# Overlapping a layer norm and its keys with the first steps of a scan, in a one-core Macaron block

## The chip, the cores and the metric

The kernel runs on one core of a Trainium2 chip. The metric is the device time of one execution, in microseconds (us), as the median of several runs. The engines are TensorE (PE in the profile, its weight loads PEld), VectorE (DVE), ScalarE (ACT), GpSimd (POOL) and SyncE (SP), each working through its own instructions in order and waiting on semaphores for the others.

## What is computed

```python
x = L0_attn_x                                   # (2, 1024, 128) f32
x = x + 0.5 * ffn(layernorm(x), router_w, w_fc, w_proj, shared_fc, shared_proj)
x = x + attn(layernorm(x), W_Q, W_KV, W1, b1, W2, b2)
x = x + 0.5 * ffn(layernorm(x), router_w, w_fc, w_proj, shared_fc, shared_proj)

def attn(x, ...):                               # a small MLP trained while it reads the tokens
    k, v = split(x @ W_KV)                      # 1024 time steps, 2 sequences
    params = scan over t: params - LR * grad(mean((mlp(params, k_t) - v_t) ** 2))
    return mlp(params, x @ W_Q)                 # mlp: silu(h @ W1 + b1) @ W2 + b2
```

The feed-forward part `ffn` sends each of the 2048 tokens to its best 2 of 8 experts, and to a shared one.

## The kernel before, in words

The 2048 tokens lie in SBUF in `res` as 16 blocks of 128 (`NBLK`), in 4 groups of 4 blocks (`NG`, `GRP`; a group is 512 columns, `COLS`). Every engine has a program written out by hand, and the order in it is the order of the work; nothing is scheduled by a tool. The program has three stages: the first feed-forward part, the scan, and the second feed-forward part.

**The end of the first feed-forward part.** GpSimd writes each token's two routed results to DRAM (`y_dram`), and SP and ScalarE read them back by group into `y_rows` (`load_results`, L534): half 0 by SP, half 1 by ScalarE; the semaphore `y_in[g]` stands at 32 when both halves of group g are there. VectorE's `add_routed` (L1640) adds both halves to `res` group by group (L1647, L1651) and takes the statistics of each group (`norm_stats`, L406). When all four groups are done it aggregates the 16 blocks (`norm_moments`, L414), works out the inverse deviation of all 16 in twelve short dependent operations (`norm_scale` and `rsqrt`, L422 and L395), and normalises the 16 blocks into `ln` (`normalise`, L427). TensorE meanwhile runs products whose result nobody reads (`pe_keep_busy`, L555): five when two groups of `res` are complete, five more when all four are.

**Keys.** A group's keys and values are made in five parts, 0 to 4 (`pe_key_part`, L863, with what the other engines do for each part in `act_key_part`, `dve_key_part` and `pool_key_part`): 0 transposes `ln` (ScalarE copies it to `ln_t`), 1 multiplies it by the key weights (ScalarE copies to `k_t`, GpSimd rounds that to `k_r`), 2 multiplies by the value weights (VectorE copies to `v_t`), 3 transposes the keys (ScalarE copies to `k_rows`), 4 multiplies each block's keys with themselves (VectorE masks the result into `kk`, GpSimd rounds it to `kk_r`).

**The scan.** It is solved by guess and correction: a chain of cheap steps (`ahead`) runs some steps ahead of an exact chain (`final`), in 16 turns of one block each. Before the turns stand three steps of the chain `ahead` alone on block 0 (`first_steps`, L964; `FIRST_AHEAD` is 3; the prediction calls them the opening steps 0, 1 and 2). An opening step is, in order: the hidden product (`pe_first`, `pe_again`), silu and tanh on ScalarE (L1150, L1158), `dve_aa`, the copies `act_guess` and `act_rows`, `dve_u` and `dve_e` on VectorE, `pool_slope` on GpSimd, and `dve_d`, which releases the next step's `pe_again`. The key parts of groups 1, 2 and 3 lie between the operations of opening steps 0, 1 and 2: `key_part(slot)` (L858) says which part stands in which of the 15 slots. After the opening steps `pe_w1_sums` (L1114) begins the updates from which the turns start.

`k_t`, `v_t`, `k_rows` and `kk` lie in `stage`, in the place that `tiles` and `y_rows` have in the feed-forward part, so `k_rows` and `kk` overlap `y_rows`:

```python
k_rows = stage[:, 2 * T:3 * T].rearrange("p (b d) -> p b d", d=P)
kk = stage[:, 3 * T:4 * T].rearrange("p (b d) -> p b d", d=P)
y_rows = stage[:, NT * ROW:NT * ROW + TOPK * T].rearrange("p (k n) -> p k n", k=TOPK)
```

## Time and profile before

| | |
|---|---|
| median of 3 runs | 511.83 us (509.27 to 514.12) |
| the profiled execution, its own time | 513.47 us |
| its span in the trace | 511.6 us |
| busy: TensorE, VectorE, ScalarE, GpSimd | 441.3, 277.3, 245.3, 233.8 us |
| mean granted clock of TensorE, as a share of 2.4 GHz | 0.948 |
| first feed-forward part, up to the last routed result | 0 to about 149 us |
| read back, add, normalise, first keys | about 149 to 175 us |
| the three opening steps | 175.07 to 192.39 us |
| turns, query, second feed-forward part | from 192.39 us |

The profile shows one execution; times in it count from the start of its span. The profiled execution's own time is 1.9 us longer than its span. Busy time is by engine and overlaps. A row of the timeline gives the start, the duration, the engine, the line, the operation with its tiles, and how many like it were merged; in brackets stands the idle time of the engine before it and what ended that. Each 512-column matmul in f32 is recorded as two, so five calls of `pe_keep_busy` are ten records.

### The profile page before, as it was taken

How to read it: one execution, taken by the hardware profiler on the slowest of the kernel's cores; microseconds unless marked ns; L12 is line 12 of the kernel's file. 1: busy time of each engine (PE TensorE's matmuls, PEld its weight loads, DVE VectorE, ACT ScalarE, POOL GpSimd, SP SyncE). 2: the span in 40 equal slices, each digit the busy share in tenths (PEclk: the TensorE clock that was granted, in tenths of full speed). 3: DMA queues.
4: the chain of work that ended last, by engine and by line, in shares of the span. 5: the costliest groups of instructions: out<-in, count | busy, mean ns of one | idle time of the engine just before them, and what ended most of it. 6: DMA issues, size and time to landing. Idle time of an engine off the chain costs nothing.

```text
span 511.6 us, 10071 instructions
## 1 busy us (share of the span) xinstructions
PE 441.3 (86%) x2962; PEld 363.6 (71%) x2962; DVE 277.3 (54%) x1045; ACT 245.3 (48%) x650; POOL 233.8 (46%) x335
## 2 busy tenths in 40 slices
PE   7896787999935999999999999999986869999950
PEld 5342477999932578999999999974532468999940
DVE  4852334555528556666666666655871443555524
ACT  2872134555530355556556556535871324555520
POOL 4176575444530033545545545551066665544430
PEclk9999999999975999999999999999998799999985
DMA  8961316101036500000000000000011316101019
GB/s 232 282 221 42 94 49 182 36 27 31 10 91 173 131 1 1 1 1 3 2 1 2 1 3 1 1 1 2 2 37 47 100 43 188 33 27 31 24 35 228
DMA packets 34515, 30.91 MB, mean 60 GB/s; under 512 B 3838, under 2 KB 30085, under 8 KB 34464
## 3 DMA queue, kind: packets, MB, share of 16 engines
q1 hardware_dynamic: 24608, 19.17, 13.7%
q0 software_dynamic: 4544, 8.47, 5.2%
q10 hardware_dynamic: 5312, 2.62, 1.9%
q8 instruction: 28, 0.46, 0.4%
q14 instruction: 23, 0.19, 0.1%
HBM read 15.55 MB, written 15.61 MB: 61 GB/s over the span
## 4 chain that ended last, share of the span: by engine, by line
PE 75%; DVE 9%; issue 5%; DMA 4%; another core or an unknown queue 3%; ACT 2%; POOL 1%; ACTq 1%; DVEq 0%; POOLq 0%
PE bank L1220 20%; PE bank L701 15%; PE bank L688 14%; PE bank L659 4%; PE bank L559 3%; DMA stage<-y_dram 3%; PE bank L649 3%; PE bank L1043 2%; PE bank L676 2%; PE bank L1108 2%; PE bank L1076 2%; PE bank L1081 2%; DVE stats L409 1%; PE bank L1102 1%
## 5 line engine op out<-in xcount | busy, mean ns | idle before, releaser
L1600 DVE TENSOR_TENSOR sq<-bank,relu 128x512 f32<-128x512 f32 x86 | 59.4, 691 | 106.5 <-ACT relu L801 73.6
L1350 POOL DMA_INDIRECT y_dram<-y_out,stage x78 | 76.4, 980 | 71.3 <-ACT y_out L827 66.1
L701 PE MATMUL bank<-proj_w,sq 128*128 x624 | 88.1, 285 | 12.1 <-DVE sq L1600 7.3
L1345 POOL DMA_INDIRECT slots_dram<-rows,slots x64 | 63.3, 989 | 67.5 <-ACT rows L752 35.4
L701 PEld LDWEIGHTS bank<-proj_w,sq 128*128 128x128 f32 x624 | 77.0, 194 | 16.7 <-issue 14.8
L688 PE MATMUL bank<-tileT,tile_w 128*128 128x128 f32 x624 | 83.9, 279 | 2.9 <-ACT tileT L793 2.8
L801 ACT ACTIVATE relu<-bank 128x512 f32<-128x512 f32 x94 | 55.8, 595 | 53.3 <-PE bank L688 25.2
L688 PEld LDWEIGHTS bank<-tileT,tile_w 128*128 128x128 f32 x624 | 77.3, 195 | 3.4 <-ACT tileT L793 3.1
L827 ACT ACTIVATE y_out<-bank,stage 128x128 f32<-128x128 f32 x78 | 28.7, 367 | 48.2 <-PE bank L701 38.2
L1215 POOL TENSOR_TENSOR sq<-sq,last_rows 128x128 f32<-128x128 f32 x32 | 14.6, 456 | 50.1 <-DVE sq L1196 50.1
L559 PE MATMUL bank<-ones 128*128 128x512 f32 x38 | 22.1, 730 | 15.5 <-DVE res L1651 12.7
L649 PE MATMUL bank<-ln_t,fc_w 128*128 128x512 f32 x64 | 32.0, 594 | 1.8 <-POOL fc_w L1356 1.8
L1618 DVE COPY tile_w<-fc_w 128x512 f32 x78 | 33.3, 429 | 0.0
L659 PE MATMUL bank<-sq,proj_w 128*128 128x512 f32 x32 | 20.1, 722 | 11.9 <-DVE sq L1600 5.9
L559 PEld LDWEIGHTS bank<-ones 128*128 128x128 f32 x38 | 8.4, 233 | 24.7 <-DVE res L1651 12.9
L1215 POOL TENSOR_TENSOR sq<-sq,ahead_rows 128x128 f32<-128x128 f32 x33 | 15.0, 456 | 19.6 <-DVE sq L1196 19.6
L659 PEld LDWEIGHTS bank<-sq,proj_w 128*128 128x128 f32 x32 | 6.4, 220 | 22.0 <-issue 11.9
L649 PEld LDWEIGHTS bank<-ln_t,fc_w 128*128 128x128 f32 x64 | 11.6, 190 | 14.6 <-issue 14.6
L1081 PE MATMUL bank<-ident,sq 128*128 128x128 f32 x65 | 18.5, 284 | 0.0
L1190 DVE SCALAR_TENSOR_TENSOR sq<-bank,b_sb,stage 128x128 f32<-128x128 f32 x32 | 11.2, 351 | 12.0 <-PE bank L1220 11.1
L659 PE MATMUL bank<-stage,proj_w 128*128 128x512 f32 x32 | 17.4, 640 | 0.0
L934 POOL CAST rounded<-stage 128x512 fp32r<-128x512 f32 x4 | 2.5, 613 | 32.1 <-ACT stage L910 32.1
(269 smaller groups left out, 1061.6 us busy)
## 6 DMA issues: line engine op xcount, KB each, us to landing
slots_dram<-pad SPq DMA_DIRECT2D x2, 2535.0 KB, 13.9
stage<-slots_dram SPq DMA_DIRECT2D x18, 260.0 KB
fc_w<-experts SPq DMA_DIRECT2D x1, 2048.0 KB, 20.3
proj_w<-experts SPq DMA_DIRECT2D x1, 2048.0 KB
stage<-y_dram SPq DMA_DIRECT2D x8, 256.0 KB, 5.5
stage<-y_dram ACTq DMA_DIRECT2D x8, 256.0 KB, 6.1
y_dram<-y_out,stage POOLq DMA_INDIRECT x78, 2.6
res<-x SPq DMA_DIRECT2D x4, 256.0 KB, 4.2
```

The source lines that it names most:

```text
L559: nc.tensor.matmul(bank[0][:], ones[:], ones[:].unsqueeze(1).to_broadcast([P, 4, P]), start=True, stop=True)
L649: nc.tensor.matmul(wide_of(i)[0][:], fc_w[:, 0, f_cols], ln_t[:, g * COLS:(g + 1) * COLS], start=True, stop=True).then_inc(fc_done, 1)
L659: nc.tensor.matmul(bank[4 + g % 2][:], proj_w[:, 0, j * P:(j + 1) * P], wide_of(i)[2], start=j == 0, stop=j == FJ - 1).then_inc(proj_done, 1)
L688: last = nc.tensor.matmul(bank[i % 2][:, f_cols], tile_w[:, i % 2, f_cols], tileT[:, (f * NQ + tile_q(i)) % 2, tile_cols(i)], start=True, ...
L701: last = nc.tensor.matmul(bank[4 + i % 2][:, 0:P], sq[:, i % 2, f_cols], proj_w[:, k, f_cols], start=j == 0, stop=j == FJ - 1)
L801: nc.scalar.activation(wide_of(i)[1], wide_of(i)[0][:], ACT.Relu).then_inc(relu_done, 1)
L1215: nc.gpsimd.tensor_tensor(x.slope, x.u, x.rows[:, 0:P].bitcast(F32), ALU.subtract).then_inc(x.slope_done, 1)
L1220: return nc.tensor.matmul(out_bank[:, 0:P], lhs_t, rhs, start=start, stop=stop)
L1345: nc.gpsimd.indirect_dma_start(to, bass.IndirectOffsetOnAxis(slots[:, n:n + 1], 0), rows[:, k, b, :], None, bounds_check=limit, oob_is_err ...
L1350: nc.gpsimd.indirect_dma_start(y_dram.ap(), bass.IndirectOffsetOnAxis(tiles[:, t, P:P + 1].bitcast(U32), 0), y_out[:, t % YBUFS, :], None, ...
L1600: nc.vector.tensor_tensor(wide_of(i)[2], wide_of(i)[0][:], wide_of(i)[1], ALU.mult)\
L1618: nc.vector.tensor_copy(tile_w[:, t % 2, :].rearrange("p (a c) -> p a c", a=1), fc_w[:, expert_of(packed, stored_as(t)), :]).then_inc(tile ...
```

## The change

In words:

- VectorE adds, measures and normalises group 0 alone (`add_group`, `norm_scale(dve, at, 0, GRP)`), then adds and measures group 1. Groups 2 and 3 are added and measured on VectorE at the end of opening step 0.
- GpSimd adds the two halves of `y_rows` of groups 1 to 3 to each other first, so that VectorE has one addition for each of these and not two.
- The inverse deviation of group 1 is worked out in pieces of three operations between VectorE's operations of opening step 0, that of groups 2 and 3 (together) between those of opening step 1. ScalarE normalises those blocks (`act_normalised`), four in opening step 0 and eight in opening step 1.
- The key parts come one opening step later: opening step 0 has parts 4 and 3 of group 0, steps 1 and 2 have groups 1 and 2, and group 3's five parts run after step 2, with nothing between them.
- ScalarE writes `k_r` of group 0 straight from PSUM. `pe_keep_busy` is called three times, from the completion of group 0, and not ten times.
- `k_rows` moves to the free half of `rows` and `kk` gets a tile of its own, so neither overlaps `y_rows`.
- SP's fill of `slots_dram` for the second feed-forward part still waits for all four groups of `res`, which are now complete at the end of VectorE's part of opening step 0.

The diff, cut to its core:

```diff
-        k_rows = stage[:, 2 * T:3 * T].rearrange("p (b d) -> p b d", d=P)
-        kk = stage[:, 3 * T:4 * T].rearrange("p (b d) -> p b d", d=P)
+        k_rows = rows[:, 1, :, 0:P]
+        kk = sb("kk", [P, NBLK, P])
...
+        def rsqrt_guess(dve, at, lo, hi):
+            X, Y, Z = rs_x[:, lo:hi], rs_y[:, lo:hi], rs_t[:, lo:hi]
+            dve.wait_ge(dve_step, at[0])
+            dve_link(dve, nc.vector.tensor_scalar(X, mv[:, lo:hi, 1], EPS, None, ALU.add), at)
             dve_link(dve, nc.vector.tensor_scalar(Z.bitcast(I32), X.bitcast(I32), 1, None, ALU.logical_shift_right), at)
             dve_link(dve, nc.vector.tensor_scalar(Y.bitcast(I32), Z.bitcast(I32), -1.0, float(0x5F3759DF),
                                                   ALU.mult, ALU.add), at)
+        def rsqrt_newton(dve, at, lo, hi):
+            X, Y, Z = rs_x[:, lo:hi], rs_y[:, lo:hi], rs_t[:, lo:hi]
+            dve_link(dve, nc.vector.tensor_tensor(Z, X, Y, ALU.mult), at)
+            dve_link(dve, nc.vector.scalar_tensor_tensor(Z, Z, -0.5, Y, ALU.mult, ALU.mult), at)
+            dve_link(dve, nc.vector.scalar_tensor_tensor(Y, Z, 1.5, Y, ALU.add, ALU.mult), at)
...
         def key_part(slot):
-            return slot % KEY_PARTS, 1 + slot // KEY_PARTS
+            if slot < KEY_PARTS:
+                return ((4, 0), (3, 0), (0, NG), (0, NG), (0, NG))[slot]
+            return slot % KEY_PARTS, slot // KEY_PARTS
...
             elif part == 1:
                 act.wait_ge(key_multiplied, key_product(part, g))
+                if g == 0:
+                    nc.scalar.copy(k_r[:, cols], bank[5][:]).then_inc(kr_done, 1)
                 nc.scalar.copy(k_t[:, cols], bank[5][:]).then_inc(kcol_done, 1)
...
             pool_tiles(0)
-            pool_key_part(pool, 1, 0)
-            pool_key_part(pool, 4, 0)
+            for g in range(1, NG):
+                cols = slice(g * COLS, (g + 1) * COLS)
+                pool.wait_ge(y_in[g], 32)
+                nc.gpsimd.tensor_tensor(y_rows[:, 0, cols], y_rows[:, 0, cols], y_rows[:, 1, cols], ALU.add)\
+                  .then_inc(y_added, 1)
...
                 act_erows(act, step, -1)
                 act_key_part(act, *key_part(5 * step.n + 3))
+                if step.n < 2:
+                    act.wait_ge(rstd_done, 2 + step.n)
+                    for b in range(GRP, 2 * GRP) if step.n == 0 else range(2 * GRP, NBLK):
+                        act_normalised(b)
                 act_key_part(act, *key_part(5 * step.n + 4))
+            for part in range(KEY_PARTS):
+                act_key_part(act, part, NG - 1)
...
+            def add_group(dve, g):
+                cols = slice(g * COLS, (g + 1) * COLS)
+                r = res[:].rearrange("p b d -> p (b d)")[:, cols]
+                if g == 0:
+                    dve.wait_ge(shared_added, NG)
+                    dve.wait_ge(y_in[0], 32)
+                    dve_link(dve, nc.vector.tensor_tensor(r, r, y_rows[:, 1, cols], ALU.add), at)
+                else:
+                    dve.wait_ge(y_added, g)
+                nc.vector.tensor_tensor(r, r, y_rows[:, 0, cols], ALU.add).then_inc(res_done, 1)
+                dve.wait_ge(res_done, g + 1)
+                norm_moments(dve, at, g, norm_stats(dve, at, g))
+
+            def dve_norm_part(dve, n, slot):
+                lo, hi = ((GRP, 2 * GRP), (2 * GRP, NBLK), (0, 0))[n]
+                if hi == 0:
+                    return
+                if slot == 0:
+                    rsqrt_guess(dve, at, lo, hi)
+                elif slot < 4:
+                    rsqrt_newton(dve, at, lo, hi)
+                    if slot == 3:
+                        norm_shift(lo, hi)
+                elif n == 0:
+                    add_group(dve, 2)
+                    add_group(dve, 3)
...
-            stats_there = add_routed(0, True)
-            for g in range(NG):
-                norm_moments(dve, at, g, stats_there)
-            normalise(dve, at)
+            add_group(dve, 0)
+            norm_scale(dve, at, 0, GRP)
+            for b in range(GRP):
+                nc.vector.tensor_scalar(ln[:, b, :], res[:, b, :], mv[:, b, 0:1], rs_y[:, b:b + 1],
+                                        ALU.subtract, ALU.mult).then_inc(ln_done, 1)
+            add_group(dve, 1)
             dve_key_part(dve, 2, 0)
-            dve_key_part(dve, 4, 0)
...
             pe_tiles(pe, 0)
-            pe.wait_ge(res_done, NG // 2)
-            pe_keep_busy(5)
-            pe.wait_ge(res_done, NG)
-            pe_keep_busy(5)
+            pe.wait_ge(res_done, 1)
+            pe_keep_busy(3)
             pe.wait_ge(params_in, 16 * 7)
             nc.tensor.transpose(bank[7][:, 0:P], wq_sb[:], ident[:]).then_inc(wqT_done, 1)
-            for part in NG_PARTS_FIRST:
+            for part in NG_PARTS_FIRST[0:3]:
                 pe_key_part(pe, part, 0)
...
+            for part in range(KEY_PARTS):
+                pe_key_part(pe, part, NG - 1)
             pe.wait_ge(vcol_done, NG)
```

Line numbers in what follows are those of each kernel's own file. First TensorE, from the end of the first feed-forward part up to the first transposes of group 1; `bank<-ones` is a call of `pe_keep_busy`, `rounded,ahead_w` the first product of opening step 0. Before:

```order
L559 MATMUL bank<-ones 128x512 x10
L1814 MATMUL bank<-ident,wq_sb 128x128
L874 MATMUL bank<-ident,rows 128x128 x4
L880 MATMUL bank<-ln_t,wkv_sb 128x512
L885 MATMUL bank<-ln_t,wkv_sb 128x512
L897 MATMUL bank<-stage 128x128 x4
L892 MATMUL bank<-ident,stage 128x128 x4
L1220 MATMUL bank<-rounded,ahead_w 128x128
```

And now:

```order
L561 MATMUL bank<-ones 128x512 x3
L1865 MATMUL bank<-ident,wq_sb 128x128
L879 MATMUL bank<-ident,rows 128x128 x4
L885 MATMUL bank<-ln_t,wkv_sb 128x512
L890 MATMUL bank<-ln_t,wkv_sb 128x512
L1227 MATMUL bank<-rounded,ahead_w 128x128
L902 MATMUL bank<-stage 128x128 x4
```

Seven of the ten calls are gone, and the products of parts 4 and 3 moved behind the first product of the scan.

Second, ScalarE between the row copies of one opening step and the silu of the next (`ahead_ed` is the copy that `act_erows` makes, `ahead_a` the silu). From opening step 1 to step 2, before:

```order
L1178 CAST ahead_ed<-bank 128x128
L913 COPY stage<-bank 128x512
L1150 ACTIVATE ahead_a<-bank,ahead_b 128x128
L1158 ACTIVATE sq<-bank,ahead_b_half 128x128
L907 COPY ln_t<-bank 128x512
```

And now:

```order
L1185 CAST ahead_ed<-bank 128x128
L920 COPY rows<-bank 128x4x128
L754 ACTIVATE rows<-res,shift,rs_y 128x128 x8
L1157 ACTIVATE ahead_a<-bank,ahead_b 128x128
L1165 ACTIVATE sq<-bank,ahead_b_half 128x128
L912 COPY ln_t<-bank 128x512
```

The eight normalisations stand ahead of the silu; from opening step 0 to step 1 four of them stand in the same place.

Third, VectorE between the last operations of opening step 0 (`ahead_ed` is `dve_d`, `ahead_ee` is `dve_ee`) and the first of step 1 (`ahead_aa`). Before:

```order
L1203 SCALAR_TENSOR_TENSOR ahead_ed<-sq,bank 128x128
L1209 TENSOR_TENSOR ahead_ee<-bank,nmask 128x128
L924 SCALAR_TENSOR_TENSOR stage<-bank,kmask 128x512
L1183 SCALAR_TENSOR_TENSOR ahead_aa<-bank,nmask 128x128
L1196 SCALAR_TENSOR_TENSOR sq<-ahead_rows,bank 128x128
```

And now, from `ahead_ee` on:

```order
L1216 TENSOR_TENSOR ahead_ee<-bank,nmask 128x128
L407 TENSOR_TENSOR rs_t<-rs_x,rs_y 128x4
L408 SCALAR_TENSOR_TENSOR rs_t<-rs_t,rs_y 128x4
L409 SCALAR_TENSOR_TENSOR rs_y<-rs_t,rs_y 128x4
L433 SCALAR_TENSOR_TENSOR shift<-mv,rs_y 128x4
L1682 TENSOR_TENSOR res<-res,stage 128x512
L414 BN_STATS stats<-res 128x6 x4
L423 BN_AGGR mv<-stats 128x2 x4
L1682 TENSOR_TENSOR res<-res,stage 128x512
L414 BN_STATS stats<-res 128x6 x4
L423 BN_AGGR mv<-stats 128x2 x4
L399 TENSOR_SCALAR rs_x<-mv 128x8
```

One masked copy made way for four short operations, two groups of additions and statistics, and (from the last row) the next three short operations, all ahead of `dve_aa` of step 1.

## Rows read from the trace of the kernel before

**Rows 1.** The page's first line: the span of the profiled execution.

```profile
span 511.6 us, 10071 instructions
```

**Rows 2.** The chain of waits in order of time (start, us, what), 150 to 171 us.

```profile
150.40 7.23 DMA stage<-y_dram
159.00 11.70 PE bank L559 x20
```

**Rows 3.** Timeline of VectorE, 153 to 171 us: additions, statistics, inverse deviation, normalisation.

```profile
153.50 0.69 DVE L1647 TENSOR_TENSOR res<-res,stage 128x512 f32<-128x512 f32 x1 [7.92 <-DMA stage<-y_dram]
155.22 0.69 DVE L1647 TENSOR_TENSOR res<-res,stage 128x512 f32<-128x512 f32 x1 [1.02 <-DMA stage<-y_dram]
...
157.65 0.69 DVE L1647 TENSOR_TENSOR res<-res,stage 128x512 f32<-128x512 f32 x1 [0.23 <-DMA stage<-y_dram]
...
162.58 0.87 DVE L409 BATCH_NORM_STATS2 stats<-res 128x6 f32<-128x128 f32 x4
163.49 1.17 DVE L418 BATCH_NORM_AGGREGATE mv<-stats 128x2 f32<-128x6 f32 x16
164.69 0.17 DVE L424 TENSOR_SCALAR rs_x<-mv 128x16 f32<-128x16 f32 x1
...
166.98 0.18 DVE L404 SCALAR_TENSOR_TENSOR rs_y<-rs_t,rs_y 128x16 f32<-128x16 f32 x1
167.20 4.20 DVE L430 TENSOR_SCALAR rows<-res,mv,rs_y 128x128 f32<-128x128 f32 x16
```

**Rows 4.** Timeline, 170 to 193 us: group 0's keys, each opening step's first product, the end.

```profile
170.64 0.60 PE L874 MATMUL bank<-ident,rows 128*128 128x128 f32 x4
...
174.92 0.69 DVE L924 SCALAR_TENSOR_TENSOR stage<-bank,kmask 128x512 f32<-128x512 f32 x1 [0.28 <-PE bank L897]
...
175.07 0.31 PE L1220 MATMUL bank<-rounded,ahead_w 128*128 128x128 f32 x1
...
180.75 0.30 PE L1220 MATMUL bank<-rounded,ahead_w 128*128 128x128 f32 x1
...
185.96 0.31 PE L1220 MATMUL bank<-rounded,ahead_w 128*128 128x128 f32 x1
...
192.39 0.46 PE L1220 MATMUL bank<-ahead_ed,stage 128*128 128x128 f32 x2 [0.98 <-DVE stage L924]
```

**Rows 5.** Timeline in opening step 1: `dve_aa`, and a group's first wide product.

```profile
182.21 0.29 DVE L1183 SCALAR_TENSOR_TENSOR ahead_aa<-bank,nmask 128x128 fp32r<-128x128 f32 x1 [0.49 <-PE bank L1220]
...
182.36 1.12 PE L880 MATMUL bank<-ln_t,wkv_sb 128*128 128x512 f32 x2
```

**Rows 6.** Timeline of three engines, 7 to 18 us: the same operations in the first feed-forward part.

```profile
7.88 0.38 DVE L418 BATCH_NORM_AGGREGATE mv<-stats 128x2 f32<-128x6 f32 x4
...
16.08 0.19 DVE L445 TENSOR_TENSOR below<-top 128x16 f32<-128x16 f32 x1
...
16.10 1.31 POOL L1356 TENSOR_TENSOR fc_w<-fc_w,relu 128x512 f32<-128x512 f32 x1 [10.03 <-ACT relu L777]
...
17.58 0.48 ACT L752 ACTIVATE rows<-res,shift,rs_y 128x128 f32<-128x128 f32 x1
17.96 0.60 ACT L758 COPY rows<-rows 128x512 f32<-128x512 f32 x1
```

**Rows 7.** TensorE's timeline at 61 us: an idle time before it.

```profile
61.30 0.94 PE L688 MATMUL bank<-tileT,tile_w 128*128 128x128 f32 x6 [2.82 <-ACT tileT L793]
```

**Rows 8.** Busy time by stretch: PE, PEld, DVE, ACT, POOL, then granted clock, DMA, GB/s.

```profile
59.00:62.00 3.00, 0.70 (x6) 0.70 (x7) 0.00 (x0) 0.97 (x2) 0.15 (x1) 1.00 0.07 22
62.50:65.50 3.00, 2.96 (x14) 2.67 (x14) 1.72 (x4) 1.19 (x2) 2.15 (x3) 0.50 0.07 22
66.00:69.00 3.00, 3.00 (x27) 2.83 (x26) 1.02 (x2) 0.96 (x2) 2.25 (x3) 1.00 0.13 44
159.00:164.00 5.00, 5.00 (x6) 2.17 (x7) 4.90 (x23) 0.00 (x0) 0.00 (x0) 0.50 0.04 15
165.00:170.00 5.00, 5.00 (x13) 2.24 (x12) 4.62 (x22) 0.00 (x0) 0.00 (x0) 1.00 1.06 292
```

60 lines of the change are left out of this document (28 added, 32 removed).

## The prediction

> **What bounds the kernel now.** I read the views in this order: the page's head for the span [rows 1], the chain of waits in order of time, then the timeline of each engine where the chain leaves dense TensorE work. The feed-forward parts and the 16 turns lie outside the change. From 150 to 192 us the chain runs through what the change touches. It holds the read-back of the routed results (7.23 us), then 11.70 us of `pe_keep_busy` up to 170.70 us [rows 2]. These ten calls are not quite a cover: VectorE has normalised the first four blocks by about 168.3 us (167.20 plus 4 of 16 parts of 4.20 us) [rows 3], so the calls end 2.3 us after the keys could start, and the rest of the stretch is VectorE's. Group 0's keys begin at 170.64, the opening steps at 175.07, 180.75 and 185.96, and the updates that end them at 192.39 us [rows 4]. Steps 0 and 1 take 5.68 and 5.21 us, step 2 with the last masked copy behind it 6.43. What counts is when the updates start: everything behind that is the same work.
>
> **The start.** Group 0 is there at 153.50 us [rows 3]; nothing in the change moves the transfers ahead of that. Alone it needs two dependent additions (0.69 each, 0.72 with the link), statistics (162.58 to 163.49: 0.91), four aggregations (0.38, 0.40 with the link) [rows 6], the twelve short operations (164.69 to 167.20: 2.51, or 0.21 each, rows 3; they become narrower, 4 columns and not 16, and I keep the price, since so short an operation is mostly fixed cost) and 4/16 of 4.20 us. Sum: 1.44 + 0.91 + 0.40 + 2.51 + 1.05 = 6.31, so 159.8 us. TensorE gets its three calls at 154.95. At the lower clock six records took 5.0 us [rows 8], so it is free at about 160.1. Group 0's transposes start near 160.3 and not at 170.64: **10.3 us gained**.
>
> **To the first scan product.** Before, this took 4.43 us. Parts 4 and 3 now come after it, and ScalarE writes `k_r` itself. What stays is transposes (0.60), a copy (0.60) [rows 6], a wide product (1.12) [rows 5] and most of a second one: 3.2 us with the links, 0.3 more for transposes at the lower clock. That gives 163.8 and not 175.07: 11.3 us gained so far.
>
> **Opening step 0.** It loses two wide products, which sat ahead of its own small ones on TensorE (some 0.9 us each), and gets 12 short VectorE operations and one more that `dve_aa`, `dve_u`, `dve_d` and ScalarE's normalisation now stand behind (13 x 0.21 = 2.7 us, part of it in waits). I take 5.0 us: step 1's first product at 168.8, 0.7 more gained. GpSimd's three additions (1.31 us each) [rows 6] start at 155.22, 157.65 and about 159.8 [rows 3] and end by 161.1; the second and third are wanted after 169 us, so they are hidden. Group 1's is ready at 156.5, wanted at 159.8.
>
> **Opening step 1.** Here the deferred work falls due. After `dve_d` of step 0 (168.6 by this count) VectorE has `dve_ee` (0.2), four short operations (0.8), then groups 2 and 3: 2 x (0.72 + 0.91 + 0.40) = 4.1, and three short ones (0.6): `dve_aa` of step 1 starts at 174.4. Before, it started 1.46 us after the step's first product [rows 4, 5], which would be 170.3. Also ahead of it in time, ScalarE's silu waits for four normalisations; their pitch is 0.38 us (17.58 to 17.96) [rows 6], so 1.5 us from 169.8 on, which is inside VectorE's delay. Of the 4.1 us about 0.5 comes back, because the wide key product runs meanwhile. The step takes 8.8 us and not 5.2: **3.6 lost**, step 2 starts at 177.6.
>
> **Opening step 2.** Silu stands behind eight normalisations, 8 x 0.38 = 3.0 us, which can't begin before VectorE's last short operations at about 178.4. It runs at 181.5 and not at 178.0: **3.4 lost**, nothing beside it.
>
> **Group 3's keys alone.** Before, they lay inside step 2. Now they start when its products end, 177.6 + 3.4 + 5.2 = 186.2, and a group alone takes 170.64 to 174.92 plus 0.69 = 4.97 us [rows 4] and some 0.4 to the updates: 191.6. Against 6.43 us, this and step 2's tail cost 4.2 more. So 11.3 + 0.7 - 3.6 - 3.4 - 4.2 = 0.8: at the full clock some **0.8 us faster**, between 0.3 and 1.9 by when the clock rises.
>
> **The clock.** Before, TensorE ran the ten calls without a gap, and the granted clock was 0.50 from 159 to 164 us and 1.00 from 165 on [rows 8], over before the keys began. Now it must rise within three calls and the first keys, and then TensorE is thinly used: by the count above it idles some 2.5 us about 169 to 171.5 and again 178 to 182, with little work around that. An idle time of 2.82 us ended at 61.30 [rows 7]; in the stretch that held it TensorE was busy 0.70 of 3.00 us, and the clock was 0.50 from 62.5 to 65.5 and back at 1.00 after dense work [rows 8]. So I expect it to fall at least once among the opening steps. The steps with key parts hold two wide products, each nearly 0.9 us longer at the lower clock and in the way of the small ones. One fall in a step with its keys costs up to 2.1 us, one that meets VectorE's delay 0.4; both together 2.6, and a late rise at the start another 1. From 0 to 4 us I take 2.5, near the double fall. Net: 2.5 - 0.8 = **1.7 us slower**.
>
> **GpSimd beside VectorE.** The trace has just one GpSimd addition beside a VectorE operation with two SBUF sources, and there both overlap (16.08 and 16.10 us) [rows 6], but VectorE's took 0.19 us and had started first. It excludes nothing. Bounds: no delay, or VectorE waiting out what is left of the second and third addition, which fall on group 0's chain; 1.3 us for the second (157.65 to 158.96) and 1.0 for the third. I take none in the sum and keep 2.3 us for the range. The Trainium skill has a rule against this change: on the page SBUF — State Buffer, section SBUF: two separate sides, a GpSimd operation and a VectorE one with two SBUF inputs exclude each other for a whole instruction. No run here shows it; by that rule the keys start about 2 us later than in my sum.
>
> **Other edits.** SP's fill of `slots_dram` starts some 10 us later, beside the opening steps; before it ran from 164 us on beside the short chain (DMA share 1.06 from 165 to 170) [rows 8], whose operations kept their 0.21 us, and it is wanted some 200 us later. Moving `k_rows` and `kk` changes no size. The last parts of group 3 delay nobody but the updates. Nothing at the second `add_routed` changes in order. The profiled execution's own time was 513.47 us, 1.64 over the median of 511.83 and within the spread of the runs; the differences are applied to the median: 511.83 + 1.7 = 513.5 us. A measurement of this kernel tells about 1%, 5.1 us, from no change.
>
> **Rivals.**
> 1. *The gain is given back and the clock stays up* through the thin stretches: 0.3 to 1.9 us faster, 510.7 us. For it: my idle times are estimates, and some products lie between them. Against: the fall behind an idle time hardly longer [rows 7, 8].
> 2. *GpSimd's additions hold off VectorE's short chain*: first keys at 162.3, three calls over 2 us before, a late rise and the falls as well: 1.7 + 1.8 = 3.5 slower, 515.3 us. For it: GpSimd has nothing else then, so it does fall on that chain. Against: no row shows such a stall.
> 3. *Slower, by the clock alone*: three calls are too few. If the clock isn't up when the first wide product starts (162 us), TensorE never gets dense work before the turns, and all opening steps run at 1.2 GHz: a group's parts are two sets of transposes (0.60 each), two wide products (1.12 each) and one of about 1.0, some 3.5 us as they overlap; for three groups that doubles and lies on the chain, 10 us, less 0.8: about 520 us, or 517 if it rises halfway. For it: the rise took between 5 and 6 us of gapless calls [rows 8], and three calls are 5.1. Against: the keys that follow at 160.3 are nearly dense too.
> 4. *Faster*: VectorE's and ScalarE's insertions fall into waits that I count as work. Then steps 1 and 2 lose 2 us and not 7: 5 + 0.8 = 5.8 faster, 506.0 us. For it: both engines are busy only about half of the span (277.3 and 245.3 of 511.6 us). Against: their programs are in order, and the inserted blocks are in one piece of 4.1 and of 3.0 us.
>
> **How the numbers follow.** Forecast (given back, with falls of the clock) 0.47 at 513.5; rival 1 0.24; rival 2 0.13; rival 3 0.08; rival 4 0.08. The forecast's own range is 511 to 516. Rivals 1 and 2 lie inside 510 to 517. With the spread of medians (runs of before lie 2.5 us to either side) 8 in 10 is 509.3 to 517.5; it leaves out most of rivals 3 and 4. Faster by over 1% is rival 4 and a little of 1: 0.09. Slower by over 1% is rival 3 and a tail of 2: 0.13. The rest, 0.78, is within 1%.
>
> **What would show each step.** In the profile after: group 0's transposes near 160.3 us; the first scan product near 163.8; the opening steps 5.0, 8.8 and, to group 3's transposes, 8.6 us long; VectorE's additions of groups 2 and 3 just ahead of `dve_aa` of step 1, and eight normalisations just ahead of the silu of step 2; the updates near 194; a granted clock of 0.50 in a stretch between 171 and 186. A first short chain over 2.8 us would speak for rival 2, a clock of 0.50 at 165 for rival 3. The prediction is wrong if the updates start outside 188 to 199 us, or if time changes outside 150 to 195 us.

## The result, and the profile after

The changed kernel takes 522.31 us (median of 4 runs, 521.43 to 523.88), the kernel before on the same chip 511.42 (median of 4, 509.27 to 514.12): a ratio of 1.020, 95% interval 1.017 to 1.023. It is slower by 2%, where 0.3% was forecast, with a range that ended at 517.5 us.

The profiled execution took 521.43 us. The page's first line, which answers to [rows 1]:

```profile
span 519.3 us, 10073 instructions
```

Four marks in TensorE's and VectorE's timelines tell where the time went: VectorE's first addition of routed results to `res`; the first product of the updates that end the opening steps; the query product, with which the turns are over; and the first transposes of the routed tiles in the second feed-forward part. The turns (updates to the query product) are 151.7 us, 152.0 before; the stretch behind the second part's tile transposes is 104.6 and 104.4. Two stretches grew: from the first addition to the updates 45.0 us, not 38.9, and from the query product to the second part's tile transposes 65.7, not 62.8.

**The short chain.** Timeline of VectorE and GpSimd, 152 to 161 us (start, duration, engine, line, operation), which answers to [rows 3]:

```profile
152.32 0.69 DVE L1679 TENSOR_TENSOR res<-res,stage 128x512 f32<-128x512 f32 x1 [8.27 <-DMA stage<-y_dram]
...
153.77 0.88 DVE L414 BATCH_NORM_STATS2 stats<-res 128x6 f32<-128x128 f32 x4
...
154.12 1.26 POOL L1368 TENSOR_TENSOR stage<-stage 128x512 f32<-128x512 f32 x1 [7.70 <-DMA stage<-y_dram]
...
155.10 0.32 DVE L399 TENSOR_SCALAR rs_x<-mv 128x4 f32<-128x4 f32 x1
...
156.06 0.16 DVE L408 SCALAR_TENSOR_TENSOR rs_t<-rs_t,rs_y 128x4 f32<-128x4 f32 x1
156.16 1.27 POOL L1368 TENSOR_TENSOR stage<-stage 128x512 f32<-128x512 f32 x1 [0.78 <-DMA stage<-y_dram]
156.25 1.20 DVE L409 SCALAR_TENSOR_TENSOR rs_y<-rs_t,rs_y 128x4 f32<-128x4 f32 x1
...
157.62 1.27 POOL L1368 TENSOR_TENSOR stage<-stage 128x512 f32<-128x512 f32 x1 [0.19 <-DMA stage<-y_dram]
157.68 1.23 DVE L408 SCALAR_TENSOR_TENSOR rs_t<-rs_t,rs_y 128x4 f32<-128x4 f32 x1
...
159.73 1.12 DVE L1713 TENSOR_SCALAR rows<-res,mv,rs_y 128x128 f32<-128x128 f32 x4
```

Three operations of the chain end where a GpSimd addition ends: L399 at 155.42 (addition until 155.38), L409 at 157.45 (157.43), L408 at 158.91 (158.89). Two of them last 1.2 us for 0.16. The statistics, with one input, run beside the first GpSimd addition at their usual length. The short chain takes 4.6 us (155.10 to 159.69) and not 2.5. In the two further profiles of the changed kernel the additions start at other moments, and other operations of the chain are the long ones: both times L407 in one (1.12 and 1.15 us), L408 and L409 at other places in the other (1.22 and 1.26).

**TensorE behind it.** Its timeline in the same kernel, 157 to 198 us, answers to [rows 4]:

```profile
157.37 1.91 PE L561 MATMUL bank<-ones 128*128 128x512 f32 x2
...
160.91 0.66 PE L879 MATMUL bank<-ident,rows 128*128 128x128 f32 x4 [1.42 <-DVE rows L1713]
162.24 1.43 PE L885 MATMUL bank<-ln_t,wkv_sb 128*128 128x512 f32 x2 [0.68 <-ACT ln_t L912]
163.46 1.92 PE L890 MATMUL bank<-ln_t,wkv_sb 128*128 128x512 f32 x2
164.39 1.09 PE L1227 MATMUL bank<-rounded,ahead_w 128*128 128x128 f32 x1
...
170.46 0.28 PE L1227 MATMUL bank<-rounded,ahead_w 128*128 128x128 f32 x1
...
173.58 1.12 PE L879 MATMUL bank<-ident,rows 128*128 128x128 f32 x4 [2.21 <-ACT rows L754]
...
197.35 0.46 PE L1227 MATMUL bank<-ahead_ed,rows 128*128 128x128 f32 x2 [0.98 <-DVE kk L931]
```

Busy time by stretch in the changed kernel (columns as in [rows 8], the granted clock third from the end):

```profile
159.50:161.00 1.50, 0.09 (x1) 0.10 (x2) 1.43 (x6) 0.27 (x1) 0.00 (x0) 0.99 0.00 0
163.00:166.30 3.30, 3.30 (x9) 1.78 (x8) 0.69 (x1) 1.23 (x3) 0.00 (x0) 0.50 0.00 0
167.00:173.00 6.00, 2.34 (x15) 1.71 (x15) 5.54 (x23) 2.56 (x8) 1.06 (x2) 1.00 0.00 0
173.50:179.90 6.40, 6.32 (x19) 4.25 (x20) 4.08 (x23) 2.18 (x7) 1.02 (x2) 0.50 0.71 214
180.00:186.00 6.00, 2.99 (x26) 2.71 (x24) 2.54 (x11) 4.58 (x13) 0.61 (x1) 1.00 0.95 201
187.00:190.00 3.00, 3.00 (x7) 1.44 (x5) 0.44 (x2) 0.58 (x1) 1.03 (x2) 0.50 0.00 0
```

Each thin stretch at 1.00 (TensorE busy 0.09 of 1.50, 2.34 of 6.00, 2.99 of 6.00 us) is followed by a dense one at 0.50, and that is where the wide products of groups 0, 1 and 2 stand. At the lower clock each takes 1.92 to 2.02 us; group 3's second one, at the full clock (193.97 us), takes 1.02. The first ones of groups 0 and 2 (1.43 and 1.68 us) lie partly ahead of the fall. The clock fell three times, not once or twice, and so it did in all three profiles of this kernel.

**Steps 1 and 2.** Timeline of VectorE and ScalarE, 171 to 187 us; the first two rows of VectorE answer to [rows 5]:

```profile
171.76 0.68 DVE L1682 TENSOR_TENSOR res<-res,stage 128x512 f32<-128x512 f32 x1
...
171.88 1.65 ACT L754 ACTIVATE rows<-res,shift,rs_y 128x128 f32<-128x128 f32 x4 [1.02 <-DVE shift L433]
...
176.32 0.29 DVE L1190 SCALAR_TENSOR_TENSOR ahead_aa<-bank,nmask 128x128 fp32r<-128x128 f32 x1
...
182.18 3.19 ACT L754 ACTIVATE rows<-res,shift,rs_y 128x128 f32<-128x128 f32 x8 [0.74 <-DVE shift L433]
185.27 0.35 ACT L1157 ACTIVATE ahead_a<-bank,ahead_b 128x128 fp32r<-128x128 f32 x1
...
186.26 0.29 DVE L1190 SCALAR_TENSOR_TENSOR ahead_aa<-bank,nmask 128x128 fp32r<-128x128 f32 x1 [3.52 <-PE bank L1227]
```

`dve_aa` of step 1 stands behind the additions and statistics of groups 2 and 3, the silu of step 2 behind eight normalisations. Both are as forecast. In addition TensorE stood idle for 2.21 us ahead of the transposes of group 1 (173.58), which wait for ScalarE's four normalisations and stand ahead of the step's own offset product. But `dve_aa` of step 1 has no idle time before it (176.32, VectorE's operation before it starts at 176.12): VectorE's own work set its start, 5.9 us behind the step's first product, not TensorE's wait. The other 5.1 us of the step lie behind `dve_aa`, at the lower clock.

### The profile page after: what moved, and what is told of

The parts are those of the page before. It is cut to its first block, busy times and chain, and to the rows that moved or that the text cites. A ratio compares the mean times of both kernels' runs of the same rounds, so it can differ in the third digit from the quotient of the medians.

```text
span 519.3 us, 10073 instructions
## 1 busy us (share of the span) xinstructions
PE 443.5 (85%) x2948; PEld 363.8 (70%) x2948; DVE 278.6 (54%) x1056; ACT 251.8 (48%) x663; POOL 237.1 (46%) x337
## 4 chain that ended last, share of the span: by engine, by line
PE 70%; DVE 12%; issue 6%; DMA 3%; ACT 3%; another core or an unknown queue 3%; POOL 1%; ACTq 0%; DVEq 0%; POOLq 0%
PE bank L1227 20%; PE bank L703 14%; PE bank L690 13%; PE bank L661 4%; DMA stage<-y_dram 2%; PE bank L651 2%; PE bank L1050 2%; PE bank L561 2%; PE bank L678 2%; PE bank L1083 2%; PE bank L1115 2%; PE bank L1088 1%; DVE stats L414 1%; PE bank L890 1%
## 5 line engine op out<-in xcount | busy, mean ns | idle before, releaser
L1352 POOL DMA_INDIRECT slots_dram<-rows,slots x64 | 63.6, 994 | 68.7 <-DVE slots L497 27.1
L1222 POOL TENSOR_TENSOR sq<-sq,last_rows 128x128 f32<-128x128 f32 x32 | 14.6, 456 | 49.9 <-DVE sq L1203 49.9
L561 PE MATMUL bank<-ones 128*128 128x512 f32 x24 | 18.8, 930 | 11.8 <-DVE res L1682 9.0
L661 PE MATMUL bank<-sq,proj_w 128*128 128x512 f32 x32 | 18.4, 664 | 7.2 <-DVE sq L1618 4.4
L754 ACT ACTIVATE rows<-res,shift,rs_y 128x128 f32<-128x128 f32 x44 | 19.8, 481 | 5.2 <-DVE shift L433 5.2
L561 PEld LDWEIGHTS bank<-ones 128*128 128x128 f32 x24 | 6.5, 293 | 18.4 <-DVE res L1682 9.2
L661 PE MATMUL bank<-stage,proj_w 128*128 128x512 f32 x32 | 18.6, 670 | 0.7 <-DVE stage L1618 0.7
## 6 DMA issues: line engine op xcount, KB each, us to landing
slots_dram<-pad SPq DMA_DIRECT2D x2, 2535.0 KB, 14.6
```

The lines of the kernel that those rows point to most:

```text
L561: nc.tensor.matmul(bank[0][:], ones[:], ones[:].unsqueeze(1).to_broadcast([P, 4, P]), start=True, stop=True)
L661: nc.tensor.matmul(bank[4 + g % 2][:], proj_w[:, 0, j * P:(j + 1) * P], wide_of(i)[2], start=j == 0, stop=j == FJ - 1).then_inc(proj_done, 1)
L1222: nc.gpsimd.tensor_tensor(x.slope, x.u, x.rows[:, 0:P].bitcast(F32), ALU.subtract).then_inc(x.slope_done, 1)
L1352: nc.gpsimd.indirect_dma_start(to, bass.IndirectOffsetOnAxis(slots[:, n:n + 1], 0), rows[:, k, b, :], None, bounds_check=limit, oob_is_err ...
```

## Experiments

The explanation under test: the loss is made by GpSimd's additions, which hold up VectorE's chain, and by TensorE's clock, which falls in the steps where TensorE has little to do. The rivals: the new places of `k_rows` and `kk`, the orders of VectorE and ScalarE by themselves, and something in the second feed-forward part. The table has the stretches of each run's profile in us (further values are of further profiled executions of the same kernel); the ratio is to the kernel before on the same chip, with its 95% interval.

| run | keys after first addition | first addition to updates | query to tile transposes | median, us | ratio |
|---|---|---|---|---|---|
| before | 17.1, 15.5 | 38.9, 37.2 | 62.8, 64.6 | 511.42 | |
| changed kernel, three profiles | 8.6, 8.4, 8.6 | 45.0, 45.9, 46.3 | 65.7, 65.6, 63.6 | 522.31, 521.74 | 1.020 [1.017, 1.023], 1.0184 [1.0142, 1.0226] |
| e1_pool_waits | 6.9, 6.3 | 41.8, 40.8 | 63.1, 62.9 | 517.97 | 1.0104 [1.0048, 1.0161] |
| e2_busy5 | 9.0 | 43.0 | 64.8 | 523.0 | 1.021 [1.0149, 1.0271] |
| e3_place | 16.8 | 38.5 | 61.0 | 513.89 | 1.0015 [0.9989, 1.004] |
| e4_before_busy, twice | 14.6, 14.6 | 36.4, 36.4 | 62.9, 61.5 | 513.81, 510.12 | 0.9989 [0.9963, 1.0015], 0.9978 [0.996, 0.9997] |
| e5_norm_later | 6.3 | 39.7 | 62.7 | 514.35 | 1.0043 [1.0022, 1.0064] |
| e6_one_each | 6.3 | 42.0 | 63.2 | 516.03 | 1.0118 [1.0049, 1.0187] |
| e7_spread | 6.3 | 38.3 | 61.7 | 511.1 | 0.9986 [0.9951, 1.002] |
| e8_calls_inside | 6.3, 6.3 | 38.2, 40.0 | 61.7, 62.9 | 512.92 | 1.0033 [1.0008, 1.0057] |
| e9_calls_and_norm | 6.3 | 37.5 | 64.9 | 511.92 | 1.0011 [0.9987, 1.0036] |
| e10_spread_calls | 6.3 | 38.4 | 64.6 | 512.4 | 1.0021 [0.9996, 1.0047] |

Before's median is 513.69 us for the runs e1 to e4, 512.32 for e5 to e8, 511.03 for e9, e10, the second run of e4 and that of the changed kernel.

### GpSimd's additions, held back (e1_pool_waits)

```diff
             pool_tiles(0)
+            pool.wait_ge(ln_done, NBLK + GRP)
             for g in range(1, NG):
```

> The changed kernel with GpSimd's three additions made to wait until VectorE has normalised group 0. In the changed kernel two short VectorE operations of group 0's chain last 1.20 and 1.23 us, each ending with a GpSimd addition, where 0.16 is usual. Theory 1 (a GpSimd addition holds off a VectorE operation with two SBUF sources): both go back to about 0.16, group 0's transposes start about 2.1 us sooner after its data are there (6.5 us and not 8.6), and TensorE's idle time between the three calls and the keys goes, so that the clock stays at 1.00 through group 0's wide products, another 2 us. The updates then start 3 to 5 us sooner after group 0's data than in the changed kernel (40.9 and not 45.0 us). Theory 2 (the long ones are something else, the clock's fall stands alone): both stay long or move to other operations, and the time is within 1 us of the changed kernel.

Timeline of VectorE and GpSimd in this run:

```profile
157.20 0.16 DVE L409 SCALAR_TENSOR_TENSOR rs_y<-rs_t,rs_y 128x4 f32<-128x4 f32 x1
...
159.78 4.18 POOL L1369 TENSOR_TENSOR stage<-stage 128x512 f32<-128x512 f32 x3 [12.10 <-DVE rows L1714]
...
161.09 1.74 DVE L1683 TENSOR_TENSOR res<-res,stage 128x512 f32<-128x512 f32 x1 [1.39 <-POOL stage L1369]
```

The short operations are back at 0.16 us and the chain at 2.4; what is held now is VectorE's addition for group 1 (1.74 us for 0.69), which is off group 0's chain. The updates come 3.3 us sooner after the first addition (4.5 between the means of all profiles) and the ratio falls by a whole per cent. That is more than the 2.2 us by which the chain shrinks. What else differs is the clock: TensorE no longer stands idle behind its calls of `pe_keep_busy`, and the clock stays up through group 0's products:

```profile
160.50:170.00 9.50, 6.46 (x33) 4.07 (x31) 8.00 (x30) 4.23 (x11) 4.52 (x5) 1.00 0.00 0
171.00:177.00 6.00, 5.27 (x17) 3.72 (x17) 4.56 (x25) 2.84 (x8) 0.35 (x1) 0.50 0.56 193
178.00:184.00 6.00, 2.81 (x25) 2.53 (x23) 2.47 (x11) 4.65 (x13) 0.61 (x1) 1.00 0.75 187
184.50:187.50 3.00, 3.00 (x7) 1.45 (x6) 0.64 (x2) 0.85 (x2) 0.41 (x1) 0.50 0.00 0
```

The falls in steps 1 and 2 are still there.

### More calls ahead of the keys (e2_busy5)

```diff
             pe.wait_ge(res_done, 1)
-            pe_keep_busy(3)
+            pe_keep_busy(5)
```

> The changed kernel with five calls of pe_keep_busy in place of three, nothing else: they end about when group 0's blocks are normalised. Theory 1 (the fall of the clock at the first keys comes from TensorE's 1.4 us idle time behind the three calls): the clock is 1.00 from about 160 us until the opening steps, group 0's wide products take 1.1 us and not 1.4 and 1.9, and the updates start 1.5 to 2.5 us sooner. Theory 2 (the clock would fall anyway, or it costs nothing because other waits are behind it): no change, or up to 0.5 us later.

TensorE's timeline:

```profile
154.28 7.60 PE L561 MATMUL bank<-ones 128*128 128x512 f32 x10 [8.90 <-DVE res L1682]
161.83 0.60 PE L879 MATMUL bank<-ident,rows 128*128 128x128 f32 x4
163.10 1.12 PE L885 MATMUL bank<-ln_t,wkv_sb 128*128 128x512 f32 x2 [0.68 <-ACT ln_t L912]
```

The wide products of group 0 run at 1.12 us, and the way to the updates is 2.0 us shorter than in the changed kernel, though the keys start later. The profiled execution took 519.37 us, 2.1 us less than the changed kernel's (521.43), on another chip, where before is 2.3 us slower (513.69 and 511.42). The median didn't fall: 1.021 with an interval of 0.006 to either side. The other three executions took 520.39, 525.62 and 526.24 us, and those of the changed kernel's second run scatter likewise, from 518.81 to 525.53. Four executions of each don't resolve 2 us. So this run shows the clock at the start and what it does to the way in one profile, not a gain in time.

### The new places alone, in the kernel before (e3_place)

```diff
-        k_rows = stage[:, 2 * T:3 * T].rearrange("p (b d) -> p b d", d=P)
-        kk = stage[:, 3 * T:4 * T].rearrange("p (b d) -> p b d", d=P)
+        k_rows = rows[:, 1, :, 0:P]
+        kk = sb("kk", [P, NBLK, P])
```

> The kernel before with only the new places of k_rows and kk. Theory 1 (the new places cost nothing): the time of before within 0.5%. Theory 2 (the loss that the opening steps don't explain, 2.7 us in the profiled pair and more in the medians, comes from the places, because the turns or the second feed-forward part read or write them more slowly): 3 to 5 us slower than before, with the turns longer than 9.54 us.

1.0015, an interval that holds 1: the places cost nothing that can be seen.

### Fewer calls in the kernel before (e4_before_busy, twice)

```diff
             pe.wait_ge(res_done, NG)
-            pe_keep_busy(5)
+            pe_keep_busy(2)
```

(with the other call count of five as it was: seven in all)

> The kernel before with seven calls of pe_keep_busy, not ten: five behind two groups and two behind four. In before they run 2.3 us beyond the moment at which the first four blocks are normalised. Theory 1 (the calls hold up the keys): group 0's transposes start up to 2.3 us sooner, the clock stays at 1.00, the time falls by 1.5 to 2.5 us. Theory 2 (VectorE's other twelve normalisations then hold up the copies of keys and values): the gain is under 0.5 us, since VectorE is free for the first copy at 171.4 us only.

> The kernel before with the changed kernel's number of products ahead of group 0's keys (7 where it has 10), once more: the first profile had the updates 36.4 us after the first add where before has 38.9, and a ratio of 0.9989 with an interval of 0.0026 to either side. Theory 1 (the 2.5 us are real): again 36.4 us, and a ratio near 0.995. Theory 2 (the fall of the clock in before is not in every execution, and nothing is gained): ratio 0.998 or above.

The updates come 36.4 us after the first addition in both profiles. Before, it was 38.9 and, in a second profile in which the clock had risen by 162 us, 37.2. The first measurement, of 10 runs, holds 1 in its interval; the second, of 12, gives 0.9978 with an upper end of 0.9997, the one interval here that lies below 1. So part of the calls lay on the path in the profiles. In the medians it is worth some 1 us at most, and only the second measurement tells it from nothing.

### Group 3's normalisations later (e5_norm_later)

On top of e1_pool_waits:

```diff
                 if step.n < 2:
                     act.wait_ge(rstd_done, 2 + step.n)
-                    for b in range(GRP, 2 * GRP) if step.n == 0 else range(2 * GRP, NBLK):
+                    for b in range((step.n + 1) * GRP, (step.n + 2) * GRP):
                         act_normalised(b)
...
                 act_rows(act, step)
+                if step.n == 2:
+                    for b in range(3 * GRP, NBLK):
+                        act_normalised(b)
```

> The run with GpSimd's additions behind the normalisations (e1_pool_waits), and ScalarE normalises group 3 not at the end of opening step 1, ahead of step 2's silu, but in step 2 behind its rows, where ScalarE stood idle for 1.6 us. Theory 1 (the silu of step 2 waits behind eight normalisations, 3.19 us, of which four are enough): step 2's silu starts 1.6 us sooner behind the shift, first product of step 2 to the updates falls from 16.0 us to about 14.4, first add to the updates from 41.8 us to about 40.2, and the time from 1.0104 of before to about 1.007. Theory 2 (what holds step 2 is the layer norm's shift coming late and the clock at 1.2 GHz, and the wait is taken up further on): the updates come no sooner than 41.5 us after the first add.

39.7 us against 41.8 and 40.8, and 1.0043 against 1.0104. Step 2, up to group 3's transposes, takes 9.3 us and not 10.4 or 10.3, so 1.0 to 1.1 us are the wait of the silu, which bought nothing. The rest of the difference lies ahead of step 2.

### One group to a step (e6_one_each)

On top of e1_pool_waits, `add_group(dve, n + 2)` at the end of steps 0 and 1, each group's inverse root in the step after, and four normalisations at the end of each step.

> The run e1_pool_waits with one group to a step: group 2 is added and measured at the end of opening step 0, group 3 at the end of step 1; each has its own inverse root in the step that follows, and four normalisations on ScalarE at that step's end, group 3's at the end of step 2. Theory 1 (step 1 is long because dve_aa stands behind 4.1 us of adds and statistics of two groups): with 2.0 us there step 1 falls from 10.6 us to about 8.6, step 2's silu comes 1.6 us sooner, but group 3's keys start about 1.5 us later behind step 2; first add to the updates about 39.8 us (41.8 in e1), time about 1.006 of before. Theory 2 (step 1 is set by the four normalisations and group 1's transposes that TensorE has ahead of the step's own products, and by the clock): step 1 stays over 10 us, and the updates come 41.5 us after the first add or later.

Step 1 falls from 10.6 to 9.7 us, between the two theories, and the updates come at 42.0, as theory 2 has it. `dve_aa` has less of VectorE's work ahead of it; it now waits 1.38 us for TensorE's product (172.28), which stands behind the transposes of the normalised rows. Group 3's transposes wait 2.37 us for its four normalisations (188.54).

### All of it rearranged (e7_spread)

Additions on VectorE alone; group 1's inverse root ahead of step 0:

```diff
             add_group(dve, 1)
+            rsqrt_guess(dve, at, GRP, 2 * GRP)
             dve_key_part(dve, 2, 0)
+            for _ in range(3):
+                rsqrt_newton(dve, at, GRP, 2 * GRP)
+            norm_shift(GRP, 2 * GRP)
```

and in each step ScalarE's four normalisations ahead of `act_erows`.

> The changed kernel rearranged: VectorE makes all additions (none on GpSimd), group 1's inverse root stands ahead of opening step 0 around the copy of v, ScalarE normalises group 1 within step 0 and groups 2 and 3 within steps 1 and 2 ahead of the copy of the transposed error, and groups 2 and 3 are added at the ends of steps 0 and 1. Theory 1 (the loss is made of places: GpSimd beside VectorE, then silu, dve_aa and TensorE's transposes behind layer norm work that could stand in idle time): group 0's transposes about 7 us after the first add, steps 0, 1 and 2 about 5.3, 6.5 and 7 us, group 3's keys about 4.5 us more, the updates about 34 us after the first add (38.9 in before, 45.0 in the changed kernel), and the time about 4 us under before: 0.992. Theory 2 (splitting the layer norm costs more in clock and links than it gains, wherever it stands): TensorE's clock falls to 1.2 GHz in steps 1 and 2 as in the changed kernel, the updates come 39 us or more after the first add, and the time is not under before.

Step 0 took 4.9 us and step 1 6.9, near what was expected; step 2 and group 3's keys 17.1 and not 11.5. In step 2 `dve_aa` (180.10) stands without idle time behind VectorE's masked copy and group 3's additions and statistics, 5.1 us after the step's first product where step 1 has 3.8. The clock falls twice, at about 169 and 179 us. Group 3's transposes (186.43) wait 1.97 us for the four normalisations behind the late shift. 38.3 us and 0.9986: the changed kernel's loss is gone, nothing is gained over before.

### Calls inside the steps (e8_calls_inside)

On top of e1_pool_waits:

```diff
                 if step.n:
                     pe_again(pe, step)
+                    pe.wait_ge(lnT_copied, NG + step.n)
+                    for _ in range(2):
+                        nc.tensor.matmul(bank[4][:], ones[:], ones[:].unsqueeze(1).to_broadcast([P, 4, P]),
+                                         start=True, stop=True)
```

> The run e1_pool_waits with two more products without a purpose (into a bank that is free) behind the second product of opening steps 1 and 2, where TensorE stands idle for 2.2 us. Theory 1 (TensorE's clock falls to 1.2 GHz in steps 1 and 2 since the engine stands idle before them, and this costs the wide products of groups 1 and 2 twice 0.9 us each): the clock stays at 1.00 from group 0's products to the updates, first add to the updates about 39 us (41.8 in e1), time about 1.005 of before. Theory 2 (the clock is not on the path of these steps, or the products get in the way): the updates come 41.5 us after the first add or later, clock up or not.

TensorE in this run:

```profile
167.99 3.19 PE L1879 MATMUL bank<-ones 128*128 128x512 f32 x4
...
172.28 1.13 PE L885 MATMUL bank<-ln_t,wkv_sb 128*128 128x512 f32 x2
```

and busy time by stretch:

```profile
167.00:170.00 3.00, 2.85 (x8) 1.63 (x8) 2.79 (x13) 1.71 (x5) 0.00 (x0) 0.51 0.00 0
171.00:179.00 8.00, 7.55 (x42) 4.84 (x41) 5.79 (x29) 4.35 (x12) 1.64 (x3) 1.00 0.89 268
179.00:190.00 11.00, 8.89 (x52) 6.07 (x50) 3.93 (x9) 6.00 (x16) 2.27 (x4) 1.00 0.17 42
```

The clock still falls once, but while the products without a purpose run, and it is back when group 1's keys begin. 38.2 us to the updates, 3.6 less than in e1_pool_waits (2.2 between the means of two profiles each), and 0.7% less time. The second profile had it fall again at about 181.5 us and 40.0 us to the updates: in two profiles there are one and two falls, where both profiles of e1_pool_waits have two in the steps. The calls don't exclude the fall.

This run also tells what the fall in step 1 costs. VectorE's timeline has

```profile
172.99 0.29 DVE L1190 SCALAR_TENSOR_TENSOR ahead_aa<-bank,nmask 128x128 fp32r<-128x128 f32 x1
```

which is 5.8 us after the step's first product (167.15), as in the changed kernel and in e1_pool_waits (5.9). Behind it the step takes 3.1 us (3.2 in the second profile), against 5.1 in the changed kernel's first profile and 4.7 and 4.2 in e1_pool_waits. The order of operations is the same, and the wide products there take 1.13 and 1.07 us instead of 1.92 and 2.02.

> The run e8_calls_inside, a second look. It had the second part at 61.7 us. Theory 1 (scatter): anything from 61 to 66 us. Theory 2 (it goes with the kernel): 61.7 us again, within half a microsecond. For the opening steps: the updates again 38.2 us after the first add, and the granted clock at 1.00 from 171 us to the updates.

### Calls and later normalisations together (e9_calls_and_norm)

> The runs e8_calls_inside and e5_norm_later in one kernel: GpSimd's additions behind the normalisations, two products without a purpose behind the second product of opening steps 1 and 2, and group 3 normalised within step 2. Theory 1 (the causes stand one after another and add up): 38.2 us from the first add to the updates in e8_calls_inside less the 1.6 to 2.1 us of e5_norm_later, 36.3 us; 38.9 in before, so the time is 2.5 us under before, ratio 0.995. Theory 2 (the clock and the wait of the silu share one time): 37.5 us or more, ratio 0.999 or above.

37.5 us and a ratio of 1.0011, as theory 2 has it: the later normalisations bring 0.7 us over the first profile of e8_calls_inside, not 1.6 or more. That the two share one time isn't shown. `dve_aa` of step 2 comes 1.2 us sooner behind the step's first product (3.85 us, 5.01 in e8_calls_inside), and 0.4 us of that is lost behind it (4.19 us to group 3's transposes, 3.81), where group 3's normalisations now stand ahead of ScalarE's copy of the keys. Against the second profile of e8_calls_inside (40.0) the gain would be 2.5 us.

### The rearranged kernel with two calls (e10_spread_calls)

> The run e7_spread with its two falls of the clock and its late shifts mended: one product without a purpose in opening step 0 ahead of the step's inner product and one in step 2 behind its second product, and in steps 1 and 2 the last two iterations of the inverse root and the shift ahead of the copy of v. Theory 1 (what is left of the loss in e7_spread is clock and normalisation behind the shift): step 1 falls from 6.9 us to about 6, step 2 with group 3's keys from 17.1 us to about 13.5, the updates come about 34 us after the first add (38.3 in e7_spread, 38.9 in before), the time about 4 us under before, ratio 0.992. Theory 2 (VectorE's additions, statistics and inverse roots are the bound of these steps by now): steps 1 and 2 are no shorter than in e7_spread by more than 1 us together, ratio 0.998 or above.

By the time (1.0021) and the way to the updates (38.4 us) it is theory 2. The clock stays up through the steps. Step 1 is no shorter (7.0 us, 6.9 in e7_spread), and step 2 with group 3's keys takes 17.1 us as there:

```profile
156.00:182.00 26.00, 20.80 (x108) 13.24 (x107) 23.19 (x94) 13.85 (x39) 4.37 (x8) 1.00 0.23 68
183.00:187.00 4.00, 3.80 (x7) 1.61 (x8) 0.16 (x1) 0.73 (x2) 0.61 (x1) 0.57 0.56 134
```

and TensorE's timeline in its steps 1 and 2 and in group 3's keys:

```profile
169.27 0.33 PE L1227 MATMUL bank<-ahead_aa,ahead_guess 128*128 128x128 f32 x1 [1.14 <-DVE ahead_aa L1190]
...
177.42 0.33 PE L1227 MATMUL bank<-ahead_aa,ahead_guess 128*128 128x128 f32 x1 [1.03 <-DVE ahead_aa L1190]
...
183.20 1.89 PE L885 MATMUL bank<-ln_t,wkv_sb 128*128 128x512 f32 x2 [0.67 <-ACT ln_t L912]
```

VectorE is busy 23.19 of 26.00 us, and in both steps TensorE waits for its `dve_aa`. With the clock up, the layer norm's additions, statistics and roots are what `dve_aa` waits for. But VectorE is not the whole of it: step 2 alone, up to group 3's transposes, is 1.7 us shorter than in e7_spread (9.7 and 11.4), and group 3's keys, to which the fall has moved, are 1.7 us longer (7.3 and 5.7). Without group 3's keys, steps 1 and 2 are 1.5 us shorter together than in e7_spread, more than theory 2 allowed, and the fall took that back.

### Does the second part go with the kernel? (r_after_again, and four more profiles)

> The changed kernel itself once more. Its median lay 10.9 us over before, while the way from the first add to the updates is 6.1 us longer in the profiles; 2.9 us lay in the second feed-forward part, whose instructions are the same. Theory 1 (those 2.9 us are the part's own variation from run to run, 61.0 to 65.7 us in nine profiles): first add to the updates again 45.0 us, the second part near 63, and the ratio between 1.012 and 1.020. Theory 2 (the change lengthens the second part too): query product to the second part's tile transposes again over 65 us, ratio 1.020.

> The kernel before, one more look. The second feed-forward part, from the query product to the second part's tile transposes, took 62.8 us in its only profile, and 61.0, 62.9 and 61.5 us in three of kernels that differ from it little. Theory 1 (the part's length scatters whatever the kernel): anything from 61 to 66 us. Theory 2 (it goes with the kernel): 61 to 63 us.

> The changed kernel, a third look. Two profiles had the second part at 65.7 and 65.6 us. Theory 1 (scatter): anything from 61 to 66 us. Theory 2 (it goes with the kernel): 65.6 us again, so that some 3 of the 10.7 us lie there, in instructions that the change doesn't touch.

> The run e1_pool_waits, a second look. It differs from the changed kernel by one wait on GpSimd, 250 us ahead of the second part, and had it at 63.1 us where the changed kernel has 65.6. Theory 1 (scatter): anything from 61 to 66 us. Theory 2 (it goes with the kernel): 63.1 us again, within half a microsecond.

The changed kernel again: 521.74 us, 1.0184 [1.0142, 1.0226]. The second part's length is 65.7, 65.6 and 63.6 us there; 62.8 and 64.6 before; 61.0, 62.9 and 61.5 in its near kin. Neither theory holds as put: profiles of one kernel differ by up to 2.1 us, and still the changed kernel's mean (65.0) is 2.4 us over that of the other five (62.6), with overlapping ranges. Three pieces can be told apart in the timelines.

The largest is again the clock. Two calls of `pe_keep_busy` (four records) stand just ahead of the tile transposes. TensorE's timeline in the changed kernel's first profile:

```profile
404.15 1.12 PE L669 MATMUL bank<-ident,y_out 128*128 128x128 f32 x4 [5.50 <-issue]
...
411.33 3.62 PE L561 MATMUL bank<-ones 128*128 128x512 f32 x4
414.75 1.31 PE L678 MATMUL bank<-ident,stage 128*128 128x128 f32 x7
```

and in its third:

```profile
411.94 1.88 PE L561 MATMUL bank<-ones 128*128 128x512 f32 x4
```

They take 3.62 us in the first and second profile, where the granted clock is 0.50, and 1.88 in the third and in all 15 profiles of the other kernels, and the transposes follow without idle time. So 1.7 us of the 65.7 and 65.6 are the clock; without them all three profiles would lie at 63.6 to 63.9, inside the range of the other five. Whether the change makes this late fall likelier, two profiles of three don't tell.

The second piece is regular: from the query product to the first statistics of the second layer norm it is 8.75 us in all profiles of before and its kin, and 9.05 in all profiles of the changed kernel and its kin. That 0.3 us wasn't traced. The third is a stall, the 5.50 us idle time above, that every profile has in one or two pieces, 5.6 to 7.5 us in sum, at a place that shifts. Its cause is not settled, and neither is whether the change lengthens it.

## Why the prediction was wrong

**The step that failed: "GpSimd beside VectorE".** It took no delay in the sum and kept 2.3 us for the range. The two bounds given there, 1.3 and 1.0 us, were the size of what happened: 1.04 us at L409, 1.07 at L408, 0.15 at L399. [Rows 6] had one pair of operations side by side, of which VectorE's was 0.19 us long and had started first, and I took the silence of the trace for an absence. The third addition also started earlier than put, 5.3 us after the first addition to `res` (157.62) and not 6.3: the 159.8 was the start of VectorE's own addition for group 3 in before, which had waited for VectorE and not for its data. The mechanism of rival 2 was real. But its price was too low, as it counted the chain alone. The keys at 160.91 are 8.6 us after the first addition and not 6.8, TensorE stood idle for 1.42 us, the clock fell just ahead of group 0's second wide product, and stayed down into step 0. Held back, the additions give 3.3 us between first profiles, 4.5 between means. The Trainium skill says this (page SBUF — State Buffer, section SBUF: two separate sides): an instruction of GpSimd that reads SBUF, once started, keeps a VectorE one with two SBUF inputs out until its end. The trace agrees: L409 and L408 have two such inputs, and each ends 0.02 us after the GpSimd addition beside it; e1_pool_waits shows it from the other side. L399 has one input and so isn't this case, though it ends 0.04 us after an addition.

**The clock: mechanism right, size too small.** 2.5 us were taken, up to 4 allowed, for one or two falls. There were three in the changed kernel, two of them without the hold of GpSimd on VectorE (e1_pool_waits). The mis-sized term is "one that meets VectorE's delay 0.4". The fall in step 1 met that delay, but it lasted past it: `dve_aa` came nearly when forecast (5.9 us after the step's first product, 5.6 forecast). Behind it the step took 5.1, 5.1 and 3.8 us in the changed kernel and 4.7 and 4.2 in e1_pool_waits, with the fall, and 3.1 and 3.2 in e8_calls_inside without: 0.6 to 2.0 us. Step 2, up to group 3's transposes, took 10.3 to 11.8 us with a fall, and 8.8 in the first profile of e8_calls_inside without: 1.5 to 3.0 us, for which up to 2.1 had been allowed. The fall at the start followed from the delayed keys; for it the range had the 1 us of a late rise. From the keys to step 1's first product it took 9.6 to 10.6 us in the changed kernel, and 8.3 in e2_busy5, where GpSimd's additions are not held back but the clock stays up: 1.3 to 2.3 us.

**The sum at full clock: about right.** The first profile of e8_calls_inside has neither GpSimd's hold on the short chain nor a fall under a group's wide products. Its stretches are 6.3 us to the keys, 3.1 to the first scan product, 5.3, 8.9 and 8.8 for the steps and 5.6 for group 3's keys, where 6.8, 3.5, 5.0, 8.8, 8.6 and 5.4 were forecast: 38.2 in all for 38.1. That it is 0.7 us shorter than the first profile of before, near the forecast 0.8, is in part luck: by the second profiles it is 2.7 us longer (40.0 and 37.2), as its clock fell once more and that of before rose earlier. In the median it is 0.3% slower. Between first profiles the loss splits into 3.3 us (GpSimd's additions, with the clock at the start) and 3.6 (the clock in steps 1 and 2) less 0.7, between means into 4.5, 2.2 and 0.9 more. Such differences between neighbours in a row of kernels add up to the whole by construction (6.1 and 7.5), so the sum is no proof of the parts.

**Single steps.** The start: 8.6 us after the first addition where 6.8 was forecast; with the additions held back 6.3 to 6.9. Step 0: 6.1 us and not 5.0, for the same reason; 5.2 to 5.3 in e1_pool_waits. Step 1: 10.9 us and not 8.8, by the fall behind `dve_aa`. The additions and statistics, put at 4.1 us, were there (171.76 to 175.67). I had not seen that TensorE's transposes of group 1 stand ahead of the step's own products and wait for ScalarE (2.21 us), but in the changed kernel that wait lay beside VectorE's work; it shows only where that work is halved (e6_one_each). Step 2: the silu behind eight normalisations was right, 3.19 us for the 3.0 taken; to group 3's transposes 10.3 us and not 8.6, by the fall there. Group 3's keys alone: 191.74 to 197.35, 5.6 us for the 5.4 taken.

**Outside the stretch.** The prediction would be wrong, it said, if time changed outside 150 to 195 us. The time is 10.7 to 10.9 us longer, the way to the updates 7.5 between the means of three profiles each (45.7; 38.2 with e3_place counted to before). Against the same three, the second part is 2.2 us longer, of which 1.2 on average are the two calls at the lower clock, and the first addition comes 1.0 us earlier, in code that the change doesn't touch. So the profiled spans differ by 8.1 us on average (520.1 and 512.0). The other 2.6 to 2.8 us lie between profiled executions and medians, and no trace shows them.

**What was weighed wrongly.** Rival 2 held GpSimd's delay and the falls together, and still came to 515.3 us: it gave the first 1.8 us net and left the falls at 2.5. Measured in its terms they were 3.3 and 3.6 between first profiles, 4.5 and 2.2 between means. Its chance of 0.13 rested on "no row shows such a stall", in a trace that has hardly a place where one could have shown. Even with both sizes right the forecast would have been near 518 us (511.8 - 0.8 + 3.3 + 3.6), since part of the loss lies outside the stretch.

## What to carry to other kernels

Work given to GpSimd is not free beside VectorE's chain of small operations: a GpSimd operation of 1.27 us that starts just ahead of a VectorE one of 0.16 us with two SBUF inputs cost the chain 1.04 and 1.07 us here, nearly all of its length. Start it behind the chain.

An overlap that starts work sooner (here 8.5 us, counted from the first addition) has its bill in the stretch it opens. Here TensorE was thinly used there, its clock fell, and each wide product took 1.9 to 2.0 us for 1.0. A fall that begins beside another engine's delay is not paid by that delay if it lasts beyond it. Count the busy share of TensorE in the new stretch before counting the gain.

A block of work for later in a program that runs in order stands ahead of everything behind it; put it in pieces where the engine waits anyway. And when all of it is in place, add up the engine: in the last version here VectorE was busy 23 of 26 us, which leaves another order of its work 3 us there at most.

## What was not expected of the hardware

Statistics, with one input, ran unhindered beside GpSimd (four in 0.88 us from 153.77, GpSimd from 154.12), while a `TENSOR_SCALAR` of 128x4 with one input was held: 0.32 us at 155.10, and 0.59 us in e1_pool_waits at 165.96, beside a GpSimd cast from 165.91 on (in the changed kernel the same operation took 0.59 us at 167.81, the cast from 167.77 on). Two kinds of VectorE operation with one SBUF input each behave differently.

```profile
165.91 0.61 POOL L945 CAST rounded<-kk 128x512 fp32r<-128x512 f32 x1 [1.96 <-DVE kk L931]
...
165.96 0.59 DVE L400 TENSOR_SCALAR rs_t<-rs_x 128x4 int32<-128x4 int32 x1
```

The clock is not the same in two executions of one kernel: before had it up from about 165 us in one profile and from 162 in the other, with the way to the updates 1.7 us shorter and the same time overall (513.47 and 513.37 us).
